# Routing split between GpSimd and VectorE, first unit turned by TensorE, and a reordered set-up in an attention and mixture-of-experts block

## The chip, the core and the metric

The kernel runs on one core of a Trainium2 chip. The core has TensorE (PE, matrix products into eight PSUM banks), VectorE (DVE), ScalarE (ACT), GpSimd (POOL, which here also issues the indirect transfers) and SyncE (SP, which issues transfers). Each engine works through its own instructions in order and waits on semaphores for the others. The metric is the device time of one execution in microseconds. One execution was recorded with a profiler, and all rows below come from it.

## What is computed

Eight sequences of 1024 tokens with 256 features go through one block. The reference, cut to what matters:

```
mod = (silu(c) @ wmod).reshape(8, 6, 1, -1);  sa, ca, ga, sb, cb, gb = mod[:, 0..5]
ga, gb = sign(g) * max(|g|, 0.25)
h = layernorm(x) * (1 + ca) + sa
x = x + ga * attention(h)          # per 64-token segment: softmax part + memory part (M, z), 16 heads
h = layernorm(x) * (1 + cb) + sb
probs = softmax(h @ router.T);  weights, indices = top_k(probs, 2);  weights /= weights.sum + 1e-6
y_e = (silu(gate) * up) @ w2[e],   gate, up = split(h @ w13[e])          # 8 experts, 256 -> 2*512 -> 256
x = x + gb * sum over the two chosen experts of weights * y_e
```

## The kernel before

**Attention.** The tokens are 64 tiles of 128 rows. A software pipeline runs over rounds: in round i every engine runs its list of stages (`program`, in `attention`), and a stage with lag n works on tile i - n. ScalarE, VectorE and GpSimd have lags of their own, so the same tile comes later in their rounds than in TensorE's. `set_up_work` puts extra work ahead of a stage in a given round, and `engine_program` walks the lists. In steady rounds all engines are filled; the first dozen rounds and the last ones are not.

**Set-up.** The six kinds of modulation come out of `wmod` in three products (`set_up_mod(e, n)`: mod0, mod1, mod2, each of 8 x 512 in f32). Each kind is split into two 16-bit halves (hi, lo) and spread over the 128 rows with small products against `of_batch` (`replicate`, 128 x 256 each). mod0, the spread of CA, mod1 and mod2 all stand ahead of the first attention tile. The spreads of B2, GA, CB and GB (32 products) stand in rounds 2 to 4 on TensorE, and the first `scores` waits for GA to be copied out of the banks that it also uses. The loads are issued at once: SyncE takes `wmod` in three pieces, x and the causal rows, ScalarE's queue the q, k and v weights, GpSimd's the router weights, masks, `wo` and the five routing tables. `scalar_weights` (line 366) turns the q, k and v weights into 16 bits once all three have landed.

**Routing.** After the last tile, VectorE ranks the experts of each token (`Part`), counts tokens per expert (`count`, line 148 writes `cnt`) and then makes 16 groups of row selectors, `rsel` (line 1247, 128 x 1024 in 16 bits, a comparison of two tensors in SBUF). TensorE uses each group for eight products (line 1344) and frees its place in a ring of four. Between group 0 and group 1 VectorE forms the tiles per expert and the slot map (lines 1252 to 1265), and after group 4 it copies `bCol`, makes `tile_at` and the eight `onto` tables (lines 1269 to 1275). Then come the table's transposes (line 1361), `tabT` (line 1285), the lookup product (line 1366) and `gidx` (line 1290), the list of rows that the gathers need. GpSimd then issues the gathers (line 1442) and SyncE the transposing transfers (line 1448) that bring a unit's rows into `xT`.

**Experts.** 75 units in 15 groups of `ORDER = "PPSPP"`: P is a pair of tiles (256 tokens), S a single tile. A pair's `gate_up` has two halves of 24 products (line 1464), its `down` has 24 (line 1541); a single has 12 in `gate_up_by_token` (line 1496) and 12 in `down`. TensorE's order in a group is p0, down(before), p1, down(p0), single, down(p1), p2, p3's first half, down(single), p3's second half, down(p2). `xT` has three places (unit u takes that of unit u - 3), gathered rows have six. GpSimd does gather(u), then scatter(u - 5), and a scatter waits until the one before it has landed. The last three chunks of `w13` (line 82, low halves) and the low halves of `w2` (line 1606, eight of them) are also made by VectorE in this stretch: the first `gate_up` waits for the former, the first `down` for the latter.

## Time and profile before

| what | us |
|---|---|
| three timed runs, median | 1270.22 |
| lowest and highest | 1270.12, 1274.2 |
| profiled execution, whole | 1279.18 |
| its span in the trace | 1277.4 |

| engine | busy in the span |
|---|---|
| TensorE products | 1129.5 us, 88% |
| weight loads | 939.8 us, 74% |
| VectorE | 895.4 us, 70% |
| ScalarE | 702.4 us, 55% |
| GpSimd | 918.1 us, 72% |

The profiled execution is 1.8 us longer than its span and 9 us longer than the median of the timed runs. The span has four stretches: set-up and filling of the pipeline (to about 60 us), attention (to about 656 us), routing (to 716 us, when the first `gate_up` starts) and the experts. A share of busy time over the whole span says little here, since each stretch has another limit. The views used are the chain that ended last, tables of stretches, and the instructions in order of time.

### The profile page before, as it was taken

What the parts mean: (1) busy time and instruction counts of PE and PEld (TensorE: products, weight loads), DVE (VectorE), ACT (ScalarE), POOL (GpSimd) and SP (SyncE); (2) the same over time, 40 slices, a digit from 0 to 9 for tenths busy, and PEclk for the clock granted to TensorE, in tenths of its full rate; (3) what the DMA queues carried; (4) which work ended last, traced back from release to release, by engine and by line L of the source; (5) the groups of instructions that cost most, each with busy time, mean ns of one, the idle gap of its engine ahead of it and who ended that gap; (6) DMA issues with size and microseconds to landing.
All of it is one profiled execution on the core that took longest, in us unless ns stands there. A gap on an engine that the chain in (4) does not pass through costs nothing. (4 is left out here: it accounts for less than half of the span.)

```text
span 1277.4 us, 52383 instructions
## 1 busy us (share of the span) xinstructions
PE 1129.5 (88%) x19163; PEld 939.8 (74%) x19163; DVE 895.4 (70%) x2388; ACT 702.4 (55%) x1407; POOL 918.1 (72%) x971
## 2 busy tenths in 40 slices
PE   4889999999999999899633499999999999999994
PEld 0677778787877777777523388888888888888883
DVE  2689999998999999999878744544444544454442
ACT  2677888888988888888633223333223323233231
POOL 3168999998999999999840457666766766677653
PEclk8699999998999999999855699999999999999997
DMA  8133344442424243333335568888897898888972
GB/s 216 47 70 82 95 137 120 117 127 88 138 84 128 88 126 100 116 109 104 113 81 183 130 117 139 139 146 147 143 134 141 141 131 132 142 157 134 133 121 33
DMA packets 214117, 154.14 MB, mean 121 GB/s; under 512 B 113339, under 2 KB 192131, under 8 KB 213747
## 3 DMA queue, kind: packets, MB, share of 16 engines
q1 hardware_dynamic: 171152, 82.25, 26.4%
q0 software_dynamic: 30720, 54.00, 26.0%
q10 hardware_dynamic: 12002, 14.54, 4.6%
q8 instruction: 167, 2.74, 1.0%
q14 instruction: 76, 0.61, 0.2%
HBM read 61.70 MB, written 43.12 MB: 82 GB/s over the span
## 5 line engine op out<-in xcount | busy, mean ns | idle before, releaser
L1464 PE MATMUL psum<-xT,xall 128*128 128x256 f16 x2880 | 327.8, 274 | 19.2 <-DMA xT<-grow 15.1
L1566 POOL DMA_INDIRECT out<-late,sidx x135 | 219.0, 1622 | 161.9 <-DVE late L1556 61.6
L1464 PEld LDWEIGHTS psum<-xT,xall 128*128 x2880 | 282.1, 98 | 55.4 <-issue 21.1
L1442 POOL DMA_INDIRECT grow<-moe_rows,gidx x135 | 145.2, 1075 | 87.1 <-DVE gidx L1290 46.3
L1472 ACT ACTIVATE sg<-psum 128x512 f32<-128x512 f32 x120 | 71.4, 595 | 223.9 <-PE psum L1464 184.9
L1477 DVE SCALAR_TENSOR_TENSOR late<-psum,sg 128x512 f32<-128x512 f32 x120 | 82.9, 691 | 150.3 <-ACT sg L1472 111.0
L1541 PE MATMUL psum<-w2s,hT 128*128 x1440 | 168.5, 274 | 3.0 <-DVE w2s L1606 2.7
L1541 PEld LDWEIGHTS psum<-w2s,hT 128*128 128x128 f16 x1440 | 141.5, 98 | 23.7 <-issue 3.5
L766 POOL TENSOR_TENSOR pT<-sc,pT 128x1024 f16<-128x1024 f32 x64 | 136.5, 2134 | 12.5 <-ACT pT L762 12.5
L1488 DVE TENSOR_TENSOR hT<-late,hT 128x512 f16<-128x512 f32 x120 | 83.2, 693 | 83.5 <-ACT hT L1484 71.0
L1484 ACT ACTIVATE hT<-late 128x512 f16<-128x512 f32 x120 | 75.6, 630 | 102.1 <-DVE late L1477 80.4
L647 PE MATMUL psum<-h1T,wqkv 128*128 128x128 f16 x1536 | 98.7, 222 | 1.0 <-DVE h1T L637 1.0
L647 PEld LDWEIGHTS psum<-h1T,wqkv 128*128 128x128 f16 x1536 | 93.4, 99 | 3.0 <-issue 1.2
L719 DVE TENSOR_REDUCE mx<-psum 128x16 f32<-128x1024 f32 x64 | 78.1, 1220 | 9.6 <-PE psum L712 8.7
L870 DVE TENSOR_TENSOR att_o<-psum,rr 64x128 f32<-64x128 f32 x256 | 73.9, 289 | 5.0 <-DVE rr L861 0.2
L922 POOL TENSOR_TENSOR xall<-xall,gat 128x256 f32<-128x256 f32 x64 | 47.1, 735 | 35.8 <-DVE gat L919 35.6
L757 ACT ACTIVATE sc<-psum 128x1024 f32<-128x1024 f32 x64 | 65.5, 1024 | 12.1 <-PE psum L750 11.4
L762 ACT ACTIVATE pT<-sc 128x1024 f16<-128x1024 f32 x64 | 67.7, 1057 | 2.0
L780 PE MATMUL psum<-mem,sig 64*64 64x68 f32 (+1 forms) x2048 | 61.6, 260 | 3.1 <-DVE sig L696 2.8
L1556 DVE SCALAR_TENSOR_TENSOR late<-psum,wrow,grow 128x256 f32<-128x256 f32 x135 | 59.4, 477 | 6.6 <-PE psum L1541 6.5
L746 PE MATMUL psum<-stk 112*64 112x64 f16 x2048 | 58.3, 199 | 5.8 <-issue 5.5
L849 PE MATMUL psum<-vs,pT 64*128 64x33 f16 x3072 | 51.1, 174 | 10.8 <-issue 8.0
(286 smaller groups left out, 2426.2 us busy)
## 6 DMA issues: line engine op xcount, KB each, us to landing
stk<-qk SPq DMA_DIRECT2D x384, 64.0 KB, 2.8
moe_rows<-hrows SPq DMA_DIRECT2D x64, 256.0 KB, 3.9
out<-xall SPq DMA_DIRECT2D x64, 128.0 KB, 3.5
raw<-in_w ACTq DMA_DIRECT2D x26, 256.0 KB, 3.4
xall<-in_x ACTq DMA_DIRECT2D x24, 256.0 KB, 4.0
raw<-in_w SPq DMA_DIRECT2D x8, 512.0 KB, 8.8
grow<-moe_rows,gidx POOLq DMA_INDIRECT x135
xT<-grow SPq DMA_TRANSPOSE x135
```

Of the source, the lines that this page charges most:

```text
L647: i = k.e.matmul(bkB[:, n * P:(n + 1) * P], wqkv[:, b_, c, n * P:(n + 1) * P], h1T[:, k.b, a, c, :], start=(c == 0 and (a, b_) == PARTS[0] ...
L719: done(k.e.tensor_reduce(mx[:, k.b, :], bkDE.rearrange("p h (n k) -> p (h n) k", k=SEG), axis=X, op=ALU.max, negate=True), "mx")
L766: done(k.e.tensor_tensor(pT[:, k.b, 1, :, :].rearrange("p n t -> p (n t)"), sc[:, k.b, :], pT[:, k.b, 0, :, :].rearrange("p n t -> p (n t) ...
L870: i = k.e.tensor_tensor(att_o[b2 * SEG:(b2 + 1) * SEG, k.b, :].rearrange("p (n w) -> p n w", w=2 * DK)[:, :, par * DK:(par + 1) * DK], de[ ...
L1442: k.e.indirect_dma_start(grow[:, k.j, q, :], None, rows_dram, at).then_inc(s_g[k.j], 16)
L1464: i = k.e.matmul(bank[:, n * LONG:(n + 1) * LONG], w13s[:, bass.ds(ex_reg * (G * 4 * I) + ((2 * c + b_) * 2 * I + col), P)], xT[:, k.x, a, ...
L1472: done(k.e.activation(sg[:, half, :], bGate[half][:, :], ACT.Silu, scale=1.0 / W_SCALE), "sg")
L1477: done(k.e.scalar_tensor_tensor(out=hf[:, half, :], in0=bUp[half][:, :], scalar=1.0 / W_SCALE, in1=sg[:, half, :], op0=ALU.mult, op1=ALU.m ...
L1484: done(k.e.activation(h_part(k, half, 0), hf[:, half, :], ACT.Copy), "hhi")
L1488: done(k.e.tensor_tensor(h_part(k, half, 1), hf[:, half, :], h_part(k, half, 0), ALU.subtract), "hlo")
L1541: i = k.e.matmul(bY[k.y][:, q * D:(q + 1) * D], hidden, w2s[:, b_, bass.ds(ex_reg * (KC * D) + n * D, D)], start=(n == 0 and (a, b_) == PA ...
L1566: k.e.indirect_dma_start(out_rows, bass.IndirectOffsetOnAxis(ap=sidx[:, n:n + 1], axis=0), yo[:, k.v, q, :], None, bounds_check=B * T - 1, ...
```

## The change

**Routing.** GpSimd forms the tiles per expert and the slot map, with its two running sums made of three shifted additions each, and makes `tile_at` and the `onto` tables; VectorE makes its 16 `rsel` groups in a row. TensorE's lookup of tile numbers moves from group 3 to group 9. ScalarE copies `bCol`, and makes half of the high parts of `w2` between the two table halves. VectorE puts four of the seven steps on `single_end` ahead of `gidx`, and the low parts of the last `w13` chunks directly behind `ex_i`.

**First unit.** Its rows are turned by eight TensorE transposes into bank 7 and one ScalarE copy, in place of two transposing transfers.

**Experts.** In each group the single's `gate_up` now comes before down(p0), p2's `gate_up` before down(p1), and p3 whole before down(single). VectorE's `weigh` calls follow. The read of a unit's expert number stands ahead of the products before it. The low halves of `w2` are made four, two and two.

**Set-up.** `wv` is loaded by SyncE behind the second piece of `wmod`. x beyond the first two segments, the causal rows and GpSimd's loads wait until q, k and v weights have landed; the five tables are issued one per round in GpSimd's rounds 10 to 14. mod2 moves to TensorE's round 2. The spreads of GA and B2 go one at a time ahead of `t1` of tiles 3 to 10, those of CB and GB ahead of `proj_v` of tiles 1 to 8, in the free halves of banks A and C; the copies out of them are eight on VectorE and eight on ScalarE, 256 wide, in place of four and four, 512 wide.

```
@@ route_vector: between the rsel groups
-            if k == 0:
-                link(e.tensor_scalar(tiles_of[:, :], cnt[:, :], (P - 1) / 2, 1.0 / P, ALU.add, ALU.mult))
...
-                for m in range(3):
-                    ins = e.tensor_copy(maps16[:, m, :, :], bc_mid(maps[0:1, m, :], P // E))
-            if k == 4:
-                e.wait_ge(s_tcol, 1)
-                link(e.tensor_copy(tile_col[:, :], bCol[:, 0:NGRP + 3]))
...
-                for i in range(NGRP):
-                    e.tensor_scalar(onto[:, i, :], number[:, 0:NW], tile_at[:, i:i + 1], None,
@@ route_gpsimd
+        def running(out, of):
+            at = of
+            for step, to in zip((1, 2, 4), (run_a[:, :], run_b[:, :], out)):
+                e.tensor_copy(to[:, 0:step], at[:, 0:step])
+                link(e.tensor_tensor(to[:, step:E], at[:, step:E], at[:, 0:E - step], ALU.add))
+                at = to
+        e.wait_ge(s_cnt, 1)
...
+        e.wait_ge(s_col, 1)
...
+            e.tensor_scalar(onto[:, i, :], number[:, 0:NW], tile_at[:, i:i + 1], None,
@@ route_scalar
+        e.wait_ge(s_tcol, 1)
+        e.activation(tile_col[:, :], bCol[:, 0:NGRP + 3], ACT.Copy).then_inc(s_col, 1)
         for half in range(2):
             e.wait_ge(s_use, NT * (half + 1))
...
+            e.wait_ge(s_2, 16 * E)
+            w2_high(range(half * 4, half * 4 + 4))
@@ the first unit
+    def x_turn_first(k):
+        k.moved(s_g, U, 0)
+        for q in range(k.nq):
+            rows = grow[:, k.j, q, 0:D].bitcast(F16)
+            for n in range(2 * G):
+                i = k.e.transpose(bTurn[:, (n * 2 + q) * P:(n * 2 + q + 1) * P], rows[:, n * P:(n + 1) * P], idh[:, :])
@@ TensorE, one group of units
+                p1.expert()
                 if before:
                     down(before)
                 gate_up(p1, 0)
+                single.expert()
                 gate_up(p1, 1)
+                gate_up_by_token(single)
+                p2.expert()
                 down(p0)
-                gate_up_by_token(single)
-                down(p1)
                 gate_up(p2, 0)
                 gate_up(p2, 1)
+                p3.expert()
+                down(p1)
                 gate_up(p3, 0)
+                gate_up(p3, 1)
                 down(single)
-                gate_up(p3, 1)
                 down(p2)
@@ set-up
         wmod_part(e, 1)
+        e.dma_start(wq32[:, :, 2 * D:3 * D], wvT.rearrange("(c p) n -> p c n", p=P)).then_inc(s_wq, 16)
         wmod_part(e, 2)
+        e.wait_ge(s_wq, 48)
         for b2 in range(2):
             x_part(e, 0, b2, slice(2, 4), s_xx)
...
+    def spread(e, n, kinds, names, bank):
+        if n == 0:
+            set_up_wait(e, "vector", "loGB")
+        part, j = divmod(n, NJ)
+        for a in range(2):
+            mm = e.matmul(bank[:, D:2 * D], of_batch[0:B, j, :], mod8s[:, a, kinds[part], :], start=(a == 0), stop=(a == 1))
...
-            set_up_wait(k.e, "vector", "GA")
+            set_up_wait(k.e, "vector", "CA23")
```

TensorE at the start of attention, before, from the first tile's q and k product on (`h` and `idf` are the first transposes, `xall,of_batch` the spreads, `mem,sig` the memory reads):

```order
8 L647 MATMUL psum<-h1T,wqkv 128x128 x24
9 L624 MATMUL psum<-idf,h 128x128
10 L625 MATMUL psum<-of_batch,shift 128x128
11 L624 MATMUL psum<-idf,h 128x128
12 L625 MATMUL psum<-of_batch,shift 128x128
13 L316 MATMUL psum<-xall,of_batch 128x256 x12
14 L780 MATMUL psum<-mem,sig 64x68 x4
15 L780 MATMUL psum<-mem,sig 64x132 x4
16 L780 MATMUL psum<-mem,sig 64x68 x4
17 L780 MATMUL psum<-mem,sig 64x132 x4
18 L656 MATMUL psum<-wqkv,h1T 128x256 x6
19 L647 MATMUL psum<-h1T,wqkv 128x128 x24
```

The same place in the changed kernel:

```order
8 L663 MATMUL psum<-h1T,wqkv 128x128 x24
9 L640 MATMUL psum<-idf,h 128x128
10 L641 MATMUL psum<-of_batch,shift 128x128
11 L640 MATMUL psum<-idf,h 128x128
12 L641 MATMUL psum<-of_batch,shift 128x128
13 L320 MATMUL psum<-xall,cs 8x512 x2
14 L797 MATMUL psum<-mem,sig 64x68 x4
15 L797 MATMUL psum<-mem,sig 64x132 x4
16 L797 MATMUL psum<-mem,sig 64x68 x4
17 L797 MATMUL psum<-mem,sig 64x132 x4
18 L673 MATMUL psum<-wqkv,h1T 128x256 x6
19 L663 MATMUL psum<-h1T,wqkv 128x128 x24
```

The twelve spreads ahead of the first memory reads have gone, and the two products of mod2 (`xall,cs`) stand there.

VectorE in the routing, before, from the end of the slot map to the copy of the turned table:

```order
1567 L1265 CAST maps<-maps 1x128 x3
1568 L1247 TENSOR_TENSOR rsel<-count,wqkv 128x1024 x4
1569 L1269 COPY tile_col<-psum 128x11
1570 L1271 TENSOR_SCALAR tile_at<-tile_col 128x8
1571 L1272 SCALAR_TENSOR_TENSOR tile_at<-tile_col,tile_at 128x8
1572 L1275 TENSOR_SCALAR onto<-number,tile_at 128x135 x8
1573 L1247 TENSOR_TENSOR rsel<-count,wqkv 128x1024 x11
1574 L1278 TENSOR_SCALAR ex_of<-iota,tend 128x75
1575 L1280 SCALAR_TENSOR_TENSOR ex_of<-iota,tend,ex_of 128x75 x6
1576 L1282 TENSOR_SCALAR past<-iota,tend 128x75
1577 L1283 TENSOR_TENSOR ex_of<-ex_of,past 128x75
1578 L1285 COPY tabT<-psum 128x1024
```

VectorE in the changed kernel, from the end of the placing on:

```order
1560 L169 CAST wqkv<-row 128x32
1561 L1269 TENSOR_TENSOR rsel<-count,wqkv 128x1024 x16
1562 L1277 TENSOR_SCALAR ex_of<-iota,tend 128x75
1563 L1279 SCALAR_TENSOR_TENSOR ex_of<-iota,tend,ex_of 128x75 x6
1564 L1281 TENSOR_SCALAR past<-iota,tend 128x75
1565 L1282 TENSOR_TENSOR ex_of<-ex_of,past 128x75
1566 L1284 COPY tabT<-psum 128x1024
1567 L1274 SCALAR_TENSOR_TENSOR ex_of<-iota,single_end,ex_of 128x75 x4
1568 L1287 CAST found<-psum 128x135
```

The map and the `onto` tables no longer stand between the `rsel` groups. GpSimd in the changed kernel holds their end, ahead of the first gathers (`grow`):

```order
725 L1393 TENSOR_TENSOR moved<-single_end,odd 128x8
726 L1394 TENSOR_TENSOR maps<-moved,tend 128x8
727 L1396 CAST maps<-maps 1x128 x3
728 L1400 TENSOR_SCALAR tile_at<-tile_col 128x8
729 L1401 TENSOR_TENSOR tile_at<-tile_at,tile_col 128x8
730 L1402 TENSOR_SCALAR tile_at<-tile_at,tile_col 128x8
731 L1404 TENSOR_SCALAR onto<-number,tile_at 128x135 x8
732 L1479 DMA grow<-moe_rows,gidx 128x520 x11
```

Before, GpSimd had nothing between the end of attention and these gathers.

## Rows read from the trace of the kernel before

**Rows 1.** The chain that ended last, shares of the span by line.
```profile
by line: PE psum L1464 23.7%; PE psum L1541 13.3%; PE psum L1496 3.0%; issue 1.2%; DMA out<-late,sidx 1.1%; POOL out L1566 0.6%; DVE rsel L1247 0.6%; DMA xT<-grow 0.5%; DVE w2s L1606 0.3%; DMA grow<-moe_rows,gidx 0.3%; DVE ex_of L1280 0.1%;
```

**Rows 2.** Stretches of the set-up: from:to, length, busy times, PEclk, DMA share, GB/s.
```profile
0.00:8.00 8.00, 1.94 (x3) 0.39 (x4) 0.17 (x1) 1.50 (x2) 7.38 (x29) 1.00 0.65 171
8.00:14.00 6.00, 3.51 (x10) 0.98 (x8) 2.32 (x9) 2.24 (x5) 0.00 (x0) 1.00 1.06 305
14.00:28.00 14.00, 6.39 (x8) 0.86 (x8) 2.92 (x11) 1.75 (x3) 1.27 (x2) 0.89 1.04 263
30.00:44.00 14.00, 11.98 (x96) 8.78 (x97) 8.16 (x21) 8.18 (x15) 1.90 (x3) 0.50 0.10 30
```

**Rows 3.** Set-up, in order of time: start, us, engine, line, what [idle before <-releaser].
```profile
6.06 3.57 PE L310 MATMUL psum<-xall,cs 128*8 128x512 f32 x4 [6.06 <-DMA xall<-in_wmod]
...
26.64 1.48 ACT L366 ACTIVATE wqkv<-xall 128x1536 f16<-128x1536 f32 x1 [10.64 <-DMA xall<-in_wvT]
...
36.65 2.74 PE L316 MATMUL psum<-xall,of_batch 8*128 8x256 f16 x12
...
48.87 0.59 ACT L663 ACTIVATE qk<-psum 128x512 f16<-128x512 f32 x1
...
52.77 1.61 PE L780 MATMUL psum<-mem,sig 64*64 64x68 f32 x32 [2.44 <-DVE sig L696]
```

**Rows 4.** Routing and first units, in order of time.
```profile
676.31 0.17 DVE L148 TENSOR_TENSOR cnt<-seen,start 128x8 f32<-128x8 f32 x1
...
681.34 0.69 DVE L1247 TENSOR_TENSOR rsel<-count,wqkv 128x1024 f16<-128x1024 f16 x1
...
688.26 1.41 DVE L1275 TENSOR_SCALAR onto<-number,tile_at 128x135 f16<-128x135 f16 x8
689.58 6.71 DVE L1247 TENSOR_TENSOR rsel<-count,wqkv 128x1024 f16<-128x1024 f16 x11
...
696.20 0.26 DVE L1278 TENSOR_SCALAR ex_of<-iota,tend 128x75 f32<-128x75 f32 x1
...
696.88 0.59 PE L1361 MATMUL psum<-idh,tab 128*128 128x128 f16 x4
...
697.57 7.67 ACT L1331 ACTIVATE w2s<-raw 128x1024 f16<-128x1024 f32 x8
...
699.06 0.69 DVE L1285 COPY tabT<-psum 128x1024 f16<-128x1024 f16 x1
...
701.80 0.23 DVE L1290 TENSOR_SCALAR gidx<-rowf 128x135 int32<-128x135 f32 x1
...
702.90 1.09 POOL L1442 DMA_INDIRECT grow<-moe_rows,gidx  x1 [46.26 <-DVE gidx L1290]
...
707.86 23.93 SPq L1448 DMA_TRANSPOSE xT<-grow  x9
708.05 3.49 DVE L82 SCALAR_TENSOR_TENSOR xall<-late,xall 128x1024 f16<-128x1024 f32 x3
...
716.01 13.19 PE L1464 MATMUL psum<-xT,xall 128*128 128x256 f16 x96 [15.12 <-DMA xT<-grow]
...
727.04 4.63 DVE L1606 SCALAR_TENSOR_TENSOR w2s<-raw,w2s 128x1024 f16<-128x1024 f32 x4
...
731.92 4.23 PE L1541 MATMUL psum<-w2s,hT 128*128 x24 [2.71 <-DVE w2s L1606]
```

**Rows 5.** GpSimd's cheapest and usual operations: one line's durations (ns min/median/max), one group.
```profile
L606 POOL TENSOR_TENSOR nmr<-nmr,rstd x16: 192/204/218, 17.2 to 559.9; 128x4 f32<-128x4 f32 x16
...
L922 POOL TENSOR_TENSOR xall<-xall,gat 128x256 f32<-128x256 f32 x64 | 47.1, 735 | 35.8 <-DVE gat L919 35.6
```

**Rows 6.** Experts: one stretch; waits (us in total, times, longest); a piece of the chain.
```profile
750.00:1250.00 500.00, 495.89 (x4370) 426.51 (x4368) 241.35 (x517) 152.99 (x253) 330.07 (x247) 1.00 0.85 138
...
POOL out L1566 <- DMA out<-late,sidx: 49.3, 22, 5.9
...
960.56 1.05 issue
```

288 lines of the change are left out of this document (162 added, 126 removed).

## The prediction

> **What bounds the kernel now.** I first read the chain that ended last [rows 1]. Its named pieces are nearly all products of the expert stretch. Attention does not show in it because there the engines pass work back and forth; I take that stretch as unchanged, since neither the stages nor their order in the steady rounds are touched. The table of stretches then shows that TensorE is busy for 495.89 of 500 us between 750 and 1250 us at full clock [rows 6], so a new order of the same products can give back at most 4.1 us there. That leaves two places where TensorE stands still and the change acts: the set-up, where attention cannot begin before the q, k and v weights are there at 26.64 us (ScalarE idle 10.64 us, released by the load of `wv`), and the stretch from the count at 676.31 us to the first `gate_up` at 716.01 us, before which TensorE waited 15.12 us [rows 3, 4].
>
> **Set-up, the weights.** From 14 to 28 us the 16 DMA engines are full (share 1.04, 263 GB/s) [rows 2]: the weights wait behind other loads, not behind their own. Counting bytes from the shapes: before `wv` can land, the changed kernel needs two pieces of `wmod` (0.52 MB each), eight pieces of x (0.13 MB each), the three weights (0.26 MB each) and 0.12 MB of small ones, 3.0 MB, or 3.5 MB if the third `wmod` piece runs beside. Before, 8 us at 171 GB/s and 6 us at 305 GB/s moved 1.37 + 1.83 = 3.2 MB by 14 us [rows 2]. So 3.0 to 3.5 MB is there at 13.4 to 15.1 us. I take 14.5, which is 12.1 us sooner than 26.64. Bounds: a gain of 9 (fewer queues at work, slower rate) to 13.
>
> **Set-up, the rest.** mod2 now stands in the first busy rounds. Its four passes take 3.6 us as mod0's did at full clock [rows 3], but between 30 and 44 us the granted clock was 0.50, the lower of the two levels (1.2 GHz) [rows 2], where they take up to 7.1 us. Twelve spreads (2.74 us) leave the same place, so the first memory read comes 0.9 to 4.4 us later. Against that, the wait of the first `scores` for GA goes, and ScalarE no longer stops for the CB spreads before it reads the second tile's q and k, which it did until 48.87 us; TensorE's next memory read at 52.77 us had waited 2.44 us for what follows from that [rows 3]. I work the chain through: mod2, hi parts, `h1T`, q and k of tile 1, sigma of tile 1. It puts that read 15.5 to 16.7 us after the end of the first tile's q and k product, where it stood about 17.2 us after it. Gain 1 (bounds -3 and +5). The spreads are as many as before (32 products), but their copies are 16 of 256 columns instead of 8 of 512; on VectorE and ScalarE that puts about 0.4 us into each of eight rounds that are no longer idle, and GpSimd's five table issues sit ahead of its stages. The same work was done before in stalls that vanish. I take a loss of 1.6, with 0 and 6 as bounds. The SyncE queue gets the causal rows and eight x pieces behind the wait for the weights; the first segment stacks queue behind them, due some 9 us later, so I cost this at nothing; if they took more than that, `scores` of tile 0 would be late by the excess. **Set-up in all: 12.1 + 1 - 1.6 = 11.5 us sooner** (bounds 5 and 15).
>
> **Routing, VectorE.** The 11 later `rsel` groups take 6.71 us, 0.61 each. Sixteen in a row from 681.34 us end at 691.1, and the next work starts there and not at 696.20: 5.1 us sooner [rows 4]. That work, nine small operations, runs from 696.20 to 699.06, 2.86 us, so to 694.0. Beside it ScalarE makes four of the `w2` copies (7.67 / 8 = 0.96 each, 3.8 us) ahead of the second table half; if the `w2` loads are there by mid-stream this ends about 2 us after TensorE's last use. Table half (0.6), transposes (0.59), `tabT` (0.69) then end at 695.4. From the end of `tabT` at 699.75 to the start of `gidx` it was 2.05 us; four `ex_of` steps (0.32 each, 1.3) now stand beside the 1.1 us of the lookup product and add 0.2. `gidx` is done at 697.9, where it was 702.03: 4.1 us sooner.
>
> **Routing, GpSimd.** Before, GpSimd was idle for 46.26 us here [rows 4], so no row shows it at this work beside VectorE. It gets 25 operations of at most 8 columns (128 in three of them), then 3 more and the 8 `onto`. The nearest row below is 0.20 us (4 columns) and above 0.735 us (256 columns) [rows 5]. From the count (676.5) to the tenth `rsel` group (687.4), behind which TensorE now stops for the map, there are 10.9 us, 0.44 for each of 25. At 0.20 plus the wait for its own semaphore they take 6 to 7 us and nothing waits. The `onto` tables, 0.2 to 0.735 each, take 1.6 to 5.9 us from about 688.5, due at 695.4; I take 0.45, 3.6, hidden. If this cover is gone, each late microsecond counts in full. VectorE's `rsel` compares two tensors in SBUF, and GpSimd's operations read SBUF too. That the two wait for one another is possible, with no row for or against. I take 1.1 us off for it. The Trainium skill, "SBUF — State Buffer", Who interferes with whom, says that a VectorE instruction with two SBUF inputs contends with a GpSimd instruction that reads SBUF, and that the one that starts later is fully blocked; no run here shows it yet. By that rule the case is the first rival, below. **Routing: 3.0 us sooner** (bounds +4.5 and -5).
>
> **First unit.** From `gidx` done (702.03) to the rows in place (707.86, when the transposing transfers start) it was 5.8 us, and to the first `gate_up` 14.0 us [rows 4]. The 5.8 stay. Instead of the transfers come eight transposes (four take 0.59, so 1.2), one ScalarE copy of 1024 columns (0.96 to 1.05, by the `w2` copies) and three hand-overs of 0.1: 8.3 us. 5.7 us sooner. `gate_up` also needs the low parts of `w13`: 3 ex_of steps, `ex_i` and 3.49 us, done 4.8 us after `gidx`. What is late next is the low part of `w2`, needed by the first `down`. Before, TensorE had done four half units in 13.19 us and then waited 2.71 us [rows 4]. VectorE's list after `gidx` is: 4.8, index work 3.8, row weights 0.4, four `w2` (4.63), first pair, two `w2` (2.3), second pair (each half about 2.1 once ready), two `w2` (2.3): 28 us after `gidx`. TensorE has then finished the single's 12 products too, at 8.3 + 13.1 + 2.6 = 24.0, and waits about 4 us. Before, `down` began 29.9 us after `gidx`; now 28.1, with 2.6 us more work behind it. 1.8 + 2.6 = **4.4 us sooner** (bounds 2 and 6).
>
> **The groups.** The stalls in the steady groups, such as 1.05 us at 960.56, stand between p2 and p3, where two `gate_up` follow each other and p3's first half needs the banks that p2's first half filled; down(p1) now stands between. Of 4.1 us at most [rows 6] I take 1.5, since GpSimd's scatters are chained nearly as tightly as TensorE and end the kernel. Bounds 0 and 4.
>
> **Sum.** 11.5 + 3.0 + 4.4 + 1.5 = 20.4 us. The span 1277.4 becomes 1257.0 and the profiled execution 1279.2 becomes 1258.8. The timed median was 9 us under the profiled execution; taking the same 20.4 us off gives 1270.2 - 20.4 = **1249.8 us**.
>
> **Rival 1: the map is late.** If each GpSimd operation first waits out an `rsel`, it takes 0.20 + 0.61 = 0.81 us, and 25 take 20.3 us: ready at 696.8, 9.4 us behind TensorE. The ring then stops VectorE too. Against it: 4.8 of the first 10.9 us lie beside short operations, not `rsel`. It decides from 0.44 us an operation. At 0.81 it takes about 9 us of the gain: 1259. Chance 0.10. The skill's rule named above would give this time.
>
> **Rival 2: little comes of the set-up.** Weights at 18 instead of 14.5, or mod2 at the low clock and 0.4 us more in each filling round with nothing given back: 5.5 us instead of 11.5, so 1256. For it is the clock of 0.50 [rows 2]; against it the idle 10.64 us. Chance 0.13.
>
> **Rival 3, slower: p2's rows come late in every group.** p2 takes the place in `xT` that p0 frees. With the new order p2 is multiplied 2.6 us sooner after p0. Its gather is issued behind the scatter of the group before's single, whose `down` ends 2.6 us later in its group. The room shrinks by 5.2 us. Scatters wait for the one before 22 times, on average 2.2 us and at most 5.9 [rows 6]. I estimate the room at about 10 us now, so some 5 are left at the mean; at 5.9 us all the time about 1 is left, and slower transfers (DMA share 0.85) could use it up. It turns the sign from 20.4 / 14 = 1.5 us in each of 14 groups; at 2 us it costs 28 us: 1278. Against it is the short stretch of idle TensorE in the same place now. Chance 0.07.
>
> **How the numbers follow.** Forecast as summed: 0.68, own range 1242 to 1257 from the bounds taken together. Better by all upper bounds, about 1240: 0.02. The rivals: 0.10, 0.13, 0.07. What a measurement can tell from no change is 0.3%, 3.8 us. The first four cases are faster by more: 0.91 after leaving 0.02 of them to within 0.3%. Slower: 0.07. The range that should hold 8 in 10 leaves out rival 3 and some of the edges: 1239 to 1261.
>
> **What would show it.** Right: the weights' conversion on ScalarE at 13 to 16 us; the second tile's memory read near 40 us; `rsel` as one run of some 10 us; the map ready before the tenth group; gap from `gidx` to the first `gate_up` near 8.3 us; TensorE idle about 4 us before the first `down`, released by `w2` on VectorE; no stall between p2 and p3. Wrong: the conversion after 18 us; `rsel` operations longer than 0.61 us or GpSimd's longer than 0.44; TensorE waiting at the lookup of tile numbers; waits at p2's first product, released by `xT`.

## The result, and the profile after

The changed kernel takes 1253.67 us (median of 4 runs, 1250.14 to 1256.63), the kernel before 1272.21 in the same job (1270.12 to 1280.91): ratio 0.9841, 95% interval 0.9805 to 0.9876. Between the medians it is faster by 18.5 us; forecast were 20.4. The ratio is not that of the two medians: by it the gain is 20.2 us. In a later job both stood on one chip again (kernel `a_again` below): 1251.77 against 1267.16, 15.4 us between the medians, ratio 0.9885 (0.9851 to 0.9918), by it 14.6 us. The two intervals meet between 0.985 and 0.988, at 16 to 19 us.

The profiled execution of the changed kernel took 1250.14 us (span 1248.2), 29 us under that of before. That pair is misleading: before's was 9 us over its median, and part of it lies in attention, whose steady rounds the change doesn't touch. So no term below rests on these two profiles alone.

Set-up after, three stretches of the table (columns as in [rows 2]), the third 500 us of the experts from 30 us behind the first `gate_up`:

```profile
14.00:28.00 14.00, 8.79 (x39) 3.97 (x37) 7.74 (x20) 8.20 (x13) 7.65 (x10) 1.00 0.82 182
30.00:44.00 14.00, 12.01 (x285) 9.63 (x289) 10.73 (x27) 9.46 (x21) 3.14 (x6) 1.00 0.41 87
718.71:1218.71 500.00, 499.73 (x4414) 431.57 (x4413) 246.88 (x524) 155.38 (x255) 336.04 (x251) 1.00 0.84 140
```

And in order of time, as in [rows 3] (L373 is the weights' conversion, L640 the first tile's transposes, L320 mod2, L797 the memory reads of the first and the second tile):

```profile
15.76 1.48 ACT L373 ACTIVATE wqkv<-xall 128x1536 f16<-128x1536 f32 x1 [1.96 <-DMA xall<-in_wkT]
...
19.76 0.45 PE L640 MATMUL psum<-idf,h 128*128 128x128 f32 x1 [3.57 <-POOL h L631]
...
22.07 2.72 PE L663 MATMUL psum<-h1T,wqkv 128*128 128x128 f16 x24 [1.02 <-DVE h1T L653]
...
25.51 1.88 PE L320 MATMUL psum<-xall,cs 128*8 128x512 f32 x4
...
30.13 0.92 PE L797 MATMUL psum<-mem,sig 64*64 64x68 f32 x32 [2.75 <-DVE xall L437]
...
36.07 0.92 PE L797 MATMUL psum<-mem,sig 64*64 64x68 f32 x32 [1.60 <-DVE sig L713]
```

The weights are there 10.9 us sooner than in [rows 3], and the second memory read starts 16.7 us sooner. 324 products run in the two stretches, 104 in [rows 2]. The chain that ended last is still made of the expert products, as in [rows 1]:

```profile
by line: PE psum L1511 25.1%; PE psum L1588 14.4%; PE psum L1543 2.9%; issue 0.6%; PE psum L1346 0.5%; POOL onto L1404 0.4%; POOL out L1613 0.4%; DMA grow<-moe_rows,gidx 0.3%; DMA out<-late,sidx 0.3%; DVE w2s L1661 0.3%; DVE late L1524 0.2%
```

New in it are GpSimd's `onto` tables, 0.4% or 5 us.

Routing and the first units after, in order of time; the rows that answer to [rows 4]:

```profile
655.83 0.17 DVE L149 TENSOR_TENSOR cnt<-seen,start 128x8 f32<-128x8 f32 x1
...
656.10 0.20 POOL L1383 TENSOR_SCALAR tiles_of<-cnt 128x8 f32<-128x8 f32 x1 [19.93 <-DVE cnt L149]
...
660.96 10.02 DVE L1269 TENSOR_TENSOR rsel<-count,wqkv 128x1024 f16<-128x1024 f16 x16
661.18 0.52 POOL L1393 TENSOR_TENSOR moved<-single_end,odd 128x8 f32<-128x8 f32 x1
...
662.38 2.02 POOL L1396 CAST maps<-maps 1x128 f16<-1x128 f32 x3
...
668.36 1.52 POOL L1400 TENSOR_SCALAR tile_at<-tile_col 128x8 f32<-128x8 f32 x1 [3.96 <-ACT tile_col L1327]
...
671.29 5.16 POOL L1404 TENSOR_SCALAR onto<-number,tile_at 128x135 f16<-128x135 f16 x8
...
673.97 0.69 DVE L1284 COPY tabT<-psum 128x1024 f16<-128x1024 f16 x1 [0.20 <-PE psum L1363]
...
676.61 1.06 PE L1368 MATMUL psum<-onto,tabT 128*128 128x135 f16 x8 [2.74 <-POOL onto L1404]
...
678.64 0.23 DVE L1290 TENSOR_SCALAR gidx<-rowf 128x135 int32<-128x135 f32 x1
...
685.55 1.03 PE L1492 MATMUL psum<-idh,grow 128*128 128x128 f16 x8 [7.88 <-DMA grow<-moe_rows,gidx]
686.68 1.02 ACT L1496 ACTIVATE xT<-psum 128x1024 f16<-128x1024 f16 x1 [9.69 <-PE psum L1492]
...
688.71 13.57 PE L1511 MATMUL psum<-xT,xall 128*128 128x256 f16 x96 [2.13 <-ACT xT L1496]
...
702.12 2.75 PE L1543 MATMUL psum<-xall,xT 128*128 x12
...
707.25 2.35 DVE L1661 SCALAR_TENSOR_TENSOR w2s<-raw,w2s 128x1024 f16<-128x1024 f32 x2
...
709.85 5.01 PE L1588 MATMUL psum<-w2s,hT 128*128 x24 [4.98 <-DVE w2s L1661]
```

The map is ready at 664.4, 3.2 us before TensorE gets to its lookup at 667.58. The `onto` tables are not ready in time: they start at 671.29 and take 0.65 us each on GpSimd, where VectorE took 0.18 [rows 4], so the lookup product starts 1.95 us behind the end of `tabT`. From the start of the count's last step to the end of `gidx` it is 23.04 us, before 25.72. The first `down` still waits for the low halves of `w2`, and now 4.98 us.

### The profile page after: what moved, and what is told of

It reads as the page before. It is cut to its first block and busy times, and to the rows that moved or that the text cites. A ratio compares the mean times of both kernels' runs of the same rounds, so it can differ in the third digit from the quotient of the medians.

```text
span 1248.2 us, 52449 instructions
## 1 busy us (share of the span) xinstructions
PE 1122.4 (90%) x19171; PEld 934.3 (75%) x19171; DVE 895.6 (72%) x2370; ACT 704.3 (56%) x1414; POOL 932.0 (75%) x1007
## 5 line engine op out<-in xcount | busy, mean ns | idle before, releaser
L797 PE MATMUL psum<-mem,sig 64*64 64x68 f32 (+1 forms) x2048 | 58.7, 252 | 4.4 <-DVE xall L437 2.7
L927 PE MATMUL psum<-wo,aT 128*128 128x256 f16 x384 | 56.2, 286 | 2.5 <-ACT aT L919 2.5
```

## The experiments

All ratios are against the kernel before on the same chip, with 95% intervals, and a gain in us beside a ratio is worked out from it. Since timed medians move from job to job (the kernel before from 1267.16 to 1272.21, the changed one from 1251.77 to 1253.67), each is read with three distances from its profile: the place of GpSimd's residual addition of tiles 0, 6 and 63 (set-up and attention), the stretch from the count's last step to the end of `gidx`, and that from there to the first `down`.

| kernel | tile 0 | tile 6 | tile 63 | count to gidx | gidx to down | down to end |
|---|---|---|---|---|---|---|
| before | 85.27 | 140.79 | 648.90 | 25.72 | 29.89 | 545.5 |
| after | 69.82 | 125.11 | 628.43 | 23.04 | 30.98 | 538.4 |
| a_again | 72.72 | 127.47 | 631.10 | 23.71 | 29.28 | 538.7 |
| e_setup | 70.39 | 126.91 | 632.38 | 25.72 | 29.79 | 547.8 |
| e_rest | 85.63 | 139.26 | 642.99 | 23.72 | 30.98 | 539.8 |
| e_loads | 79.81 | 133.68 | 637.78 | 25.73 | 29.62 | 542.7 |
| e_mod2 | 69.34 | 125.23 | 629.27 | 23.70 | 30.95 | 538.5 |
| e_oldloads | 82.83 | 138.74 | 644.60 | 23.03 | 30.04 | 537.6 |
| e_group | 69.55 | 124.59 | 628.26 | 23.71 | 29.70 | 554.2 |
| e_onto | 70.73 | 126.07 | 627.95 | 22.85 | 28.88 | 538.4 |
| e_map | 72.56 | 127.66 | 628.05 | 25.80 | 29.60 | 538.2 |
| e_noturn | 73.35 | 128.55 | 631.38 | 23.05 | 33.41 | 541.3 |
| e_w2 | 69.61 | 124.94 | 626.83 | 23.09 | 24.90 | 535.7 |
| e_best | 72.62 | 127.80 | 630.00 | 21.50 | 24.66 | 538.6 |

### The two halves apart

`e_setup` is the kernel before with all of the diff's set-up part, `e_rest` with all of its routing and expert part.

> The kernel before with the whole new set-up and its old routing and experts. Theory A (the set-up gives more than forecast, because TensorE's products run short about 20 us sooner): the first segment's memory read of round 7 stands 16 us sooner than before (106.3 to 90.0 us, as in the changed kernel) and the time is 15 to 17 us under the kernel before, ratio 0.987 to 0.988. Theory B (the forecast, 11.5 us): ratio 0.991; the 5 us more in the profile of the changed kernel would then be the luck of one profiled execution of before, 9 us over its median. The weights' conversion on ScalarE stands at 15 to 16 us by both.

> The kernel before with its old set-up and all of the new routing, first unit and order of the groups. Theory A: set-up and rest add up, and the traces show 2.7 us sooner at gidx and 6 us sooner from there to the end, so 8 to 9 us under the kernel before, ratio 0.993. Theory B: the timed medians differ by 18.5 us only; if the set-up gives 16, the rest gives 2 to 3 us, ratio 0.998. Forecast: 8.9 us, ratio 0.993.

`e_setup`: 1261.51 against 1270.64, ratio 0.9927 (0.9899 to 0.9954), 9.3 us. `e_rest`: 1266.73, ratio 0.9959 (0.9933 to 0.9986), 5.2 us (1.8 to 8.5). Together 14.5 us, beside 14.6 and 20.2 of the changed kernel: the halves add up as far as this can be told. Theory A for the set-up falls by the time. The 16 us of the profile shrink on the way: 15 at tile 0, 12.3 at tile 6, 10.6 at tile 63, against `e_rest`, which has the old set-up. That is one pair of profiles, though; by the means over all profiles with the new and with the old set-up the distance is 14.2, 13.5 and 16.6 us, so a loss behind tile 6 is not shown. `e_rest` shows also how far a profile of the same code strays: it has before's set-up and attention and is 5.9 us ahead of before's profile at tile 63.

### What shortened the set-up

Four kernels, each with one part. `e_loads`: the order of loads alone, on the kernel before.

```
+        e.dma_start(wq32[:, :, 2 * D:3 * D], wvT...)      # SyncE, behind wmod piece 2
         wmod_part(e, 2)
+        e.wait_ge(s_wq, 48)                               # SyncE, ahead of x beyond segment 2
...
+        e.wait_ge(s_wq, 48)                               # GpSimd, ahead of its loads
         for dst, src in later_loads:
```

> The kernel before with the order of its loads alone changed: wv behind the second piece of wmod, x beyond the first two segments, causal rows and GpSimd's loads behind the weights. mod2, the spreads and the tables' place in the program are as before. Theory A: the conversion of the weights comes 10 to 11 us sooner (at about 16 us instead of 26.6), TensorE's spell of slow products (2.7 us for the 24 of a q and k product instead of 1.5) ends sooner by as much, and the time falls by 10 to 11 us, ratio 0.992; the 12 spreads ahead of the first memory read still cost 2.7 us. Theory B: mod2 ahead of the first tile holds TensorE until the third piece of wmod has landed, the first product of q and k waits for it, and the gain is 5 us or less.

1264.89, ratio 0.9955 (0.9930 to 0.9980), 5.7 us. That is near the amount of theory B, but by neither theory's mechanism: the weights come at 15.95, yet the first transposes wait for something else.

```profile
15.95 1.49 ACT L369 ACTIVATE wqkv<-xall 128x1536 f16<-128x1536 f32 x1 [1.93 <-DMA xall<-in_wkT]
...
23.23 1.09 ACT L613 ACTIVATE h<-xall,nmr,rstd 128x256 f32<-128x256 f32 x2 [5.79 <-POOL nmr L609]
...
41.87 0.60 ACT L386 ACTIVATE mods<-psum 128x512 f32<-128x512 f32 x1 [4.48 <-PE psum L319]
...
43.19 0.58 ACT L666 ACTIVATE qk<-psum 128x512 f16<-128x512 f32 x1
```

I had put GpSimd's wait and its nine loads ahead of its first stages, and ScalarE waited 5.79 us for GpSimd's `nmr` behind them. So the first transposes start at 24.85 (before 30.64, after 19.76). In the changed kernel the loads stand in GpSimd's tenth round, and the tables one to a round: half of what the earlier weights are worth hangs on that. The second thing is below it: ScalarE stops 4.48 us for a CB spread and only then reads the second tile's q and k, at 43.19; the second memory read comes at 47.09, 22.2 us behind the first transposes, as before (22.1), though many products around it run short. In the changed kernel it is 16.3.

`e_oldloads` keeps the new places of mod2 and the spreads, with the old loads; `e_mod2` is the changed kernel with mod2 back ahead of the first tile.

```
     def tensor_third(e):                                   # e_mod2: in tensor_first again
-        set_up_mod(e, 2)
```

> The changed kernel with the old order of loads (wv third on ScalarE's queue, x, causal rows and all of GpSimd's loads at once); mod2 and the spreads stay in their new places. It asks what shortened the way from the first tile's transposes to the second memory read from 22.1 us to 16.3. Theory A (the spreads, and ScalarE's and VectorE's stops for them): it stays at 16 to 17.5 us though the weights come at 26.6 and TensorE idles for them, and the first rounds are 10 to 11 us later than in the changed kernel at the end of set-up; ratio 0.993. Theory B (TensorE's clock, 0.50 in that stretch before): it goes back to 20 us or more.

> The changed kernel with mod2 back ahead of the first tile; the new loads and spreads stay. Theory A: the wait for the third piece of wmod, which now lands behind wv, costs little, since TensorE idles for the weights anyway, and mod2 no longer stands (1.88 us) between the first q and k products and the first memory read: within 2 us of the changed kernel, ratio 0.983 to 0.985 against before. Theory B: the move of mod2 is what brought the 5 us above the forecast: ratio 0.988.

`e_oldloads`: 1262.75 against 1267.16, ratio 0.9956 (0.9936 to 0.9976), that is what `e_rest` has, so the new spreads alone give nothing that can be timed. Its rows, and behind them those of `a_again`, which is the changed kernel itself:

```profile
30.57 0.45 PE L638 MATMUL psum<-idf,h 128*128 128x128 f32 x1 [10.72 <-POOL h L629]
...
36.57 2.73 PE L318 MATMUL psum<-xall,cs 128*8 128x512 f32 x4
```

```profile
19.86 0.45 PE L640 MATMUL psum<-idf,h 128*128 128x128 f32 x1 [3.91 <-POOL h L631]
...
25.87 2.64 PE L320 MATMUL psum<-xall,cs 128*8 128x512 f32 x4
...
38.54 0.92 PE L797 MATMUL psum<-mem,sig 64*64 64x68 f32 x32 [1.56 <-DVE sig L713]
```

From the first transposes to the second memory read: 18.8 us in `e_oldloads` (read at 49.37), 18.7 in `a_again`, 16.3 in the profiles of after, `e_mod2` and `e_w2`, 16.5 in `e_setup`. So 3.3 us of the 5.8 come from the spreads and the stops for them, shown by the old loads with the new spreads; the other 2.4 us come and go between executions of the same code, with TensorE's pace: mod2 takes 1.88 us in one and 2.64 in the other, and between 30 and 35 us the granted clock is 1.00 in after and 0.66 in `a_again`. The ten profiles with the new set-up fall into these two levels, six at 16.3 to 16.6 us and four at 18.6 to 18.9. `e_mod2`: 1255.27, ratio 0.9897 (0.9857 to 0.9936), which fits both theories (0.983 to 0.985 and 0.988); the profile decides. Its first memory read comes 9.1 us behind the first transposes, against 10.4 to 11.6 with mod2 in its new place, but the second at the same 16.3, and tile 0 is 0.5 us sooner than after. By the profiles the place of mod2 is worth nothing. At tile 6 `e_oldloads` is only 0.5 us ahead of `e_rest`, from 2.8 at tile 0: the rounds that carry the spreads give it back.

### Routing

`e_onto`: `tile_at` and `onto` on VectorE behind the sixteenth `rsel`. `e_map`: the map as well, between the `rsel` groups as before.

```
@@ route_vector (e_onto), taken out of route_gpsimd
+        e.wait_ge(s_col, 1)
+        link(e.tensor_scalar(tile_at[:, :], tile_col[:, 0:NGRP], whole, step, ALU.is_ge, ALU.mult))
...
+            e.tensor_scalar(onto[:, i, :], number[:, 0:NW], tile_at[:, i:i + 1], None, ALU.is_equal)
```

> The changed kernel with tile_at and the eight onto tables back on VectorE, in one piece behind the sixteenth rsel group; GpSimd keeps the map. In the changed kernel the lookup product waited 2.74 us for GpSimd's onto tables, which took 5.16 us beside VectorE where VectorE took 1.41. Theory A (GpSimd's small operations are stretched by VectorE's): the tables are ready before tabT, the lookup product starts 0.1 us behind tabT, and gidx is 1.6 to 1.9 us sooner after the count (21.0 us instead of 22.8). Theory B: VectorE, now with 1.7 us more ahead of ex_of, makes tabT late by as much, and nothing is gained. On the time 1 to 2 us of 1254, under what the timing can tell.

> The changed kernel with the whole slot map and the onto tables back on VectorE between the rsel groups and the lookup of tile numbers behind group 3, as before; all the rest as in the changed kernel. Theory A: GpSimd takes 5.1 us off VectorE's line and gives 2.4 us of it back as wait for its tables, so gidx comes 2.5 to 3 us later after the count than in the changed kernel (25.4 us instead of 22.8), time up by 2 to 3 us. Theory B (contention is large): rsel runs faster with GpSimd idle, 0.60 us instead of 0.63 each, and the loss is under 1.5 us.

```profile
670.98 1.41 DVE L1283 TENSOR_SCALAR onto<-number,tile_at 128x135 f16<-128x135 f16 x8
...
675.16 0.69 DVE L1292 COPY tabT<-psum 128x1024 f16<-128x1024 f16 x1
...
675.91 1.09 PE L1376 MATMUL psum<-onto,tabT 128*128 128x135 f16 x8 [2.73 <-DVE tabT L1292]
```

`e_onto`: 1250.26 against 1269.16, ratio 0.9852 (0.9822 to 0.9881). The tables take 1.41 us instead of 5.16 and the product starts 0.06 us behind the end of `tabT`, but `tabT` itself now stands behind `ex_of` and is 1.7 us late (it ended 18.8 us behind the count in after, 20.5 here). So 22.85 us instead of 23.03 to 23.72 (two levels, explained below): both theories hold in part, and the gain is 0.2 to 0.9 us. `e_map`: 1251.90, ratio 0.9869 (0.9838 to 0.9901). Its 25.80 us against 23.04 and 23.71 are the worth of GpSimd's share, 2.1 to 2.8 us, a little under theory A's 2.5 to 3; 25.80 is also what the kernel before has (25.72), so the other edits of the routing bring nothing up to `gidx` by themselves. With GpSimd idle `rsel` takes 6.71 / 11 = 0.61 us, with it 10.02 / 16 = 0.626. The difference lies in three of the sixteen, which start 0.69 us apart instead of 0.60, beside GpSimd's three copies of the map (662.38 to 664.40). Against theory B, VectorE hardly pays for the sharing. The times can't tell these kernels apart; the profiles do.

### First unit

`e_noturn`: the first unit's rows by two transposing transfers again.

```
-            x_turn_first(unit(e, 0))          # TensorE
-            x_copy_first(unit(e, 0))          # ScalarE
-                if k and u > 0:
+                if k:                          # SyncE
                     x_trans(k)
```

> The changed kernel with the first unit's rows brought by two transposing transfers on SyncE, as before, in place of the eight products and the copy. Theory A: the first gate_up comes later (14 us after gidx instead of 9.8), but VectorE's list of low halves of w2 ends when it did, about 30 us after gidx, because it waits for the products only in part: of 4.2 us, 2 to 4 us reach the first down and the end. Theory B: the first down is set by the w2 low halves alone, and the time doesn't change (within 0.5 us at the first down).

1256.66, ratio 0.9892 (0.9863 to 0.9920). The first `gate_up` starts 14.12 us after `gidx` instead of 9.84, the first `down` 33.41 after it instead of 29.28 to 30.98: 2.4 to 4.1 of 4.3 us arrive, as in theory A. The time can't tell it from the changed kernel (0.9841 and 0.9885).

`e_w2` asks for the wait before the first `down`. It changes VectorE's order alone:

```
+            w2_low(range(E))                   # all eight, behind the last w13 chunks
...
                 hidden(p0, 1)
+                if group == 0:
+                    index_work(e)              # oh_tile ... sidx, 11 operations
+                    row_weights(p0)
```

> The changed kernel with one order changed on VectorE: all eight low halves of w2 directly behind the last w13 chunks, and the list of scatter rows (15 operations, 3.8 us) and the first row weights behind the first pair's hidden halves. Theory A (TensorE's 5.0 us before the first down is VectorE's list): the low halves are done 14 us after gidx instead of 30.7, the first down starts behind the single's twelve products, 26 us after gidx instead of 31.0, with no wait for w2, and the time falls by 4 to 5 us (ratio 0.981). Theory B (the products are the limit): the first pair's hidden halves come later behind 4.6 us more of w2, the second half of p1 waits for its bank, and less than 2 us is won.

1249.09 against 1267.16 (`a_again` beside it 1251.77), ratio 0.9843 (0.9812 to 0.9873).

```profile
681.76 9.17 DVE L1664 SCALAR_TENSOR_TENSOR w2s<-raw,w2s 128x1024 f16<-128x1024 f32 x8
...
687.11 12.70 PE L1514 MATMUL psum<-xT,xall 128*128 128x256 f16 x96 [2.12 <-ACT xT L1499]
...
699.64 2.75 PE L1546 MATMUL psum<-xall,xT 128*128 x12
...
702.23 2.78 PE L1591 MATMUL psum<-w2s,hT 128*128 x24
```

The wait is gone and the first `down` starts 24.9 us after `gidx`. And its 24 products take 2.78 us at a granted clock of 1.00, where they took 5.01 behind the wait of 4.98, at 0.50: the stop had cost twice. By the profile the gain is 4.4 to 6.1 us up to the first `down` and some 3 us behind it; the medians say 2.7 and the ratios 5.3, with intervals that overlap, so that the size isn't settled by timing. The profiled execution, 1239.83 us, is also the fastest of its six, 9 us under their median.

### The groups

`e_group`: the old order of products on TensorE and of `weigh` on VectorE, the reads of the expert numbers as in the change.

```
                 gate_up(p1, 1)
+                down(p0)
                 gate_up_by_token(single)
-                down(p0)
+                down(p1)
                 gate_up(p2, 0)
                 gate_up(p2, 1)
-                down(p1)
                 gate_up(p3, 0)
-                gate_up(p3, 1)
                 down(single)
+                gate_up(p3, 1)
```

> The changed kernel with the old order of products in a group on TensorE and of weigh on VectorE; the reads of the expert numbers stay ahead. Theory A (the stalls between p2 and p3 are what the new order removes): between 30 and 530 us behind the first gate_up TensorE is busy 496 of 500 us instead of 499.7, and the time is 3.5 to 4 us over the changed kernel. Theory B (the early reads of the expert numbers do it): TensorE stays busy for over 499 us and the time is the same within 1 us.

1252.83, ratio 0.9864 (0.9835 to 0.9894): by the time no difference from the changed kernel. Its profiled execution is the slowest of its seven, 1265.23, and shows where such an execution loses its time. TensorE in 500 us of the experts, from 30 us behind the first `gate_up`, for `e_group`, then `e_setup` (old order) and `a_again` (new order):

```profile
719.11:1219.11 500.00, 487.46 (x4294) 418.52 (x4293) 237.34 (x509) 151.25 (x247) 325.24 (x248) 1.00 0.86 138
```

```profile
729.05:1229.05 500.00, 493.14 (x4338) 423.14 (x4337) 240.60 (x516) 153.72 (x252) 331.53 (x247) 1.00 0.85 138
```

```profile
721.98:1221.98 500.00, 499.66 (x4413) 431.35 (x4411) 245.79 (x525) 155.88 (x254) 331.32 (x252) 1.00 0.83 139
```

The waits of `e_group` in this stretch (us in total, times, longest), TensorE's first, then GpSimd's, and behind them GpSimd's in the changed kernel:

```profile
PE psum L1511 <- DMA xT<-grow: 11.0, 7, 3.3
```

```profile
POOL out L1613 <- DMA out<-late,sidx: 87.4, 42, 5.7
```

```profile
POOL out L1613 <- DMA out<-late,sidx: 51.2, 21, 4.9
```

Of its 12.5 us of idle TensorE 11.0 are waits for rows in `xT`: here GpSimd waited for scatters twice as often as in the changed kernel, its gathers came late, and so did the rows. That is no stall of the order, so this profile doesn't price it. The other three with the old order have 495.48 (before), 495.85 (`e_loads`) and 493.14 us busy; ten with the new one 497.7 to 500.0, the changed kernel among them with 499.73 and 499.66. The groups themselves tell the same: from ScalarE's first copy for the single of the second group to that of the fifteenth it is 464.7 to 466.4 us in the three and 459.4 to 463.0 in the ten. I read 4 to 5 us from that; the timed pair (1252.83 against 1251.8 to 1253.7 for the changed kernel) doesn't confirm it.

### What a better order gives

`e_best` is `e_w2` with `tile_at` and `onto` on VectorE, `tabT` ahead of the last half of the first `ex_of` steps, and all steps on `single_end` behind `gidx`.

```
+        by_pair(range(1, 4))
         e.wait_ge(s_made, 3)
         e.tensor_copy(tabT[:, :, :], ...).then_inc(s_tabT, 1)
+        by_pair(range(4, E - 1))
...
         e.tensor_scalar(gidx[:, :], rowf[:, :], 0.0, None, ALU.max).then_inc(s_idx, 1)
-        by_single(range(4, E - 1))
+        by_single(range(0, E - 1))
```

> The kernel of the run before it with, in addition, tile_at and the onto tables on VectorE behind the sixteenth rsel group, tabT ahead of half of the first ex_of steps, and all steps on single_end behind gidx. Theory A: with the tables back, only the place of tabT holds up the lookup product (VectorE made tabT 1.2 us late behind ex_of in the kernel with onto alone moved); gidx comes 21.5 to 22 us after the count instead of 23.0 to 23.7, and with the 5 us from w2 the time is 6 to 7 us under the changed kernel, about 1246, ratio 0.980. Theory B: the twelve other ex_of steps behind gidx delay the first gate_up by the w13 low halves and give the routing's gain back.

> The changed kernel unchanged, so that the other kernels of this job stand beside it on one chip: ratio 0.985 against before, routing from the count to gidx 23.0 to 23.7 us, first down 31.0 us after gidx.

```profile
673.02 1.41 DVE L1283 TENSOR_SCALAR onto<-number,tile_at 128x135 f16<-128x135 f16 x8
...
675.63 0.69 DVE L1292 COPY tabT<-psum 128x1024 f16<-128x1024 f16 x1
...
676.38 1.09 PE L1381 MATMUL psum<-onto,tabT 128*128 128x135 f16 x8 [1.11 <-DVE tabT L1292]
...
703.55 2.78 PE L1593 MATMUL psum<-w2s,hT 128*128 x24
```

1242.46 against 1267.16, ratio 0.9797 (0.9765 to 0.9828); the changed kernel in the same job 0.9885 (0.9851 to 0.9918). These intervals don't meet: it beats both kernels, the changed one by 9 us between the medians and 11 by the ratios. From the count to `gidx` it is 21.50 us and from there to the first `down` 24.66, together 6.8 us less than in `a_again`, within the 6 to 7 us expected. All seven steps on `single_end`, four more than in the change, now stand behind `gidx` (not twelve more, as expected above), and they hold up nothing: the first `gate_up` comes 9.0 us after `gidx`, in `a_again` 9.8.

## Why the prediction was right, and where it wasn't

The time and the sign were right: 1249.8 forecast, 1253.67 measured, 20.4 us against 18.5 and 15.4 between the medians. That the sum came so close is in part luck: set-up and groups gave more than forecast in the profiles, routing and first unit less. The own range of 1242 to 1257 doesn't follow from the bounds either; added one by one they reach from 1241 to 1268. By its steps, each measured by the stage (means over all profiles that have the part: for set-up the residual addition of tile 6, 140.0 in two with all of the old set-up against 126.6 in nine with all of the new; for the groups TensorE's busy time in 500 us, 494.8 against 499.2; for the first unit the first `down`, 29.77 us after `gidx` in three profiles of the old kind against 30.10 in the seven with both the turned rows and the new order, and the 2.6 us of work behind it):

| term | forecast | measured |
|---|---|---|
| weights there | 12.1 (14.5 us) | 10.9 (15.76 us) |
| set-up in all | 11.5 | 13.5 in profiles, 9.3 timed |
| count to gidx | 3.0 | 2.35 |
| gidx to first gate_up | 5.7 | 4.2 |
| first unit in all | 4.4 | 2.3 |
| groups | 1.5 | about 4 in profiles |

**Weights.** The bytes counted gave 13.4 to 15.1 us; the last of the three weights to land was k's, at 15.76, not v's, so it wasn't the queue of the moved load. 1.2 us late.

**Set-up, the rest.** The mechanism was right (fewer stops of ScalarE before the second tile's q and k), its size wasn't: +1 was taken, with +5 as a bound; the runs show 3.3 us from the spreads. I had the second memory read 15.5 to 16.7 us after the end of the first q and k product; it is 11.3 us in after and 13.7 in `a_again`. The step that failed is mod2's price: I put it at 3.6 to 7.1 us, since I took mod0's 3.6 us for TensorE's full pace. In its new place it took 1.88 to 2.85 us; 3.57 is the price at the lower level, as the last section shows. The first memory read still came 1.3 to 2.5 us later behind the first transposes (9.1 before), inside the 0.9 to 4.4 forecast, but for another reason: TensorE is done with mod2 at 27.39 and then waits 2.75 us for VectorE, which works on mod2's results. That this number fits is luck. The loss of 1.6 us by later rounds is there: 14.2 to 16.7 us at the second memory read are 13.5 at tile 6. What I named in one sentence without a price, that GpSimd's tables stand ahead of its stages, was the larger matter: badly placed, GpSimd's loads cost 5.1 us in `e_loads`.

**Routing.** Sixteen `rsel` in 10.02 us, as forecast. GpSimd's map took 0.18 to 0.26 us an operation beside VectorE's short ones (once 0.35) and 0.52 to 0.67 beside `rsel`: 8.3 us in all, 0.33 each, where the first rival decides from 0.44. 20 of the 25 were through before the first `rsel` got in their way. What followed was mis-sized: the three `tile_at` steps took 1.52, 0.47 and 0.68 us, and the tables 0.65 each for 0.45. They were due at the end of `tabT` and late by 1.95 us. The length of the tables alone would not have done it, since I had covered up to 5.9 us for the eight and they took 5.16. But I had them start 7.2 us after the first `rsel`, and they started 10.3 us after it, behind the `tile_at` steps.

The first of these steps is the costly one, and it has two lengths: 1.52 us in four profiles (after, `e_oldloads`, `e_noturn`, `e_w2`) and 2.91 to 2.92 in the four others (`a_again`, `e_rest`, `e_mod2`, `e_group`). These are the four with 23.03 to 23.09 us from the count to `gidx` and the four with 23.70 to 23.72. From `a_again`, that step, and the last two tables:

```profile
671.02 2.92 POOL L1400 TENSOR_SCALAR tile_at<-tile_col 128x8 f32<-128x8 f32 x1 [3.96 <-ACT tile_col L1327]
```

```profile
L1404 POOL TENSOR_SCALAR onto<-number,tile_at x2: 617/620/622, 678.6 to 679.2; 128x135 f16<-128x135 f16 x2
```

The step stands beside a run of `rsel` on VectorE. The two after it, behind the end of that run, take 0.20 and 0.35 us. If 0.20, 0.20 and 0.35 are taken as GpSimd's own price, the three steps are stretched by 1.9 us in after and 2.7 in `a_again`, and the lookup product is late by 1.95 and 2.71. That is an account from rows; no run has these steps on GpSimd with `rsel` elsewhere. The two tables above stand beside an idle VectorE (from 678.44 to 681.11), so 0.62 us is GpSimd's own price at 135 columns, and little of the 0.65 comes from VectorE at work beside it.

**Rival 1** was right about contention and wrong about what it hits: beside `rsel` most operations took 0.52 to 0.67 us, not 0.81, on the map nothing waited, and the tables were late instead. So the two signs named for it, `rsel` over 0.61 us and GpSimd's operations over 0.44, did show, and the loss was 2 to 3 us at the lookup product instead of the 9 priced. The Trainium skill, "SBUF — State Buffer", Who interferes with whom, says that of a VectorE instruction with two SBUF inputs and a GpSimd one that reads SBUF the later is blocked in full. By these rows the direction agrees: 8 columns on GpSimd go from 0.20 to 0.52 us, and for the first `tile_at` step to 1.52 or 2.92, more than one `rsel`. But VectorE, which by the rule would be blocked whenever it comes second, lost 0.016 us on each `rsel` in the mean and 0.1 at most; and its six `ex_of` steps, which have two inputs in SBUF too, take 1.96 us beside GpSimd's tables, as they did before without them. That side of the rule these rows don't bear out.

**First unit.** Three hand-overs were taken at 0.1 us. The last one, from ScalarE's copy to the first `gate_up`, takes 1.0 us (687.70 to 688.71). In the trace TensorE's sequencer loads the unit's expert number there, from 687.74 to 688.23, and computes with it until 688.65: for the first unit this read stands behind the wait. The gather was seen 0.8 us later on TensorE than on SyncE. Then the first `down`: forecast 28.1 us after `gidx`, measured 28.9 to 31.0, 30.1 in the mean, which with 2.6 us more work behind it makes the 2.3 of the table. The list on VectorE was right in its order; I had it end at 28 and it ended at 30.7, as `gate_up` came 1.5 us later. What I left out is that TensorE runs slowly behind such a wait (5.01 us for 24 products at a granted clock of 0.50, 2.78 without the wait at 1.00).

**Groups.** I took 1.5 of 4.1 us because GpSimd's scatters seemed nearly as tight as TensorE. In the profiled executions with the new order they mostly aren't; TensorE is idle for 0.3 of 500 us after.

**Rival 2** did not come: the weights were there before 18 us. **Rival 3** did not either: the changed kernel waits at most 0.3 us for `xT` in 500 us of the groups, and the most in a kernel with the new order is 2.3 us (`e_noturn` and `e_best`). Rows that come late are real, though: `e_group`'s profile shows them in one execution, 11.0 us in 7 waits, and `e_best`'s 2.5 us in 2. But `e_group` has the old order, so this is not the room that rival 3 has the new order take away.

Still open: the terms by stage add up to 13.5 + 2.35 + 2.3 + 4 = 22.2 us, and the timed runs give 15 to 20. `e_rest` and `e_setup` come out lower timed than by their stages as well (5.2 for 8.7, 9.3 for 13.5, which is above the 12.8 that the interval of `e_setup` allows). Each stage was seen in two to ten profiled executions. What takes the difference back, or whether two profiles with the old set-up are too few, these runs don't tell.

## What to carry to other kernels

When loads are full, count the bytes ahead of the one that everything waits for; but then look at which engine issues the loads put back and what stands behind them, since a wait there can eat half the gain. Small serial work is well placed on an idle GpSimd as long as it has slack beside VectorE's long operations (a step of 0.2 us took 1.5 to 2.9 there); what is due at a fixed point (here eight tables of 135 columns) is cheaper on VectorE, placed behind the copy that the next engine waits for. Before a first product, make everything that it needs and nothing that is needed later: in the profiles the order of one list on VectorE was worth at least as much as the whole routing change, in the times 2.7 to 5.3 us.

## What the runs showed of the hardware

**The clock column reads 1.00 where nothing is recorded.** In the changed kernel's profile it stands at 1.00 from the first product on, and yet mod0 takes 3.57 us and the first 24 q and k products 2.72, as long as the same 24 before at a granted clock of 0.50 (1.2 GHz, [rows 2]); ten microseconds later 24 take 1.50. But this trace has no clock record ahead of 24.9 us, and the column shows 1.00 for want of one. In `e_group` the records begin at 8.4 us, and there the same 24 products stand at 0.50:

```profile
21.80:24.60 2.80, 2.78 (x25) 2.65 (x25) 0.91 (x3) 2.40 (x5) 1.80 (x4) 0.50 0.98 187
```

```profile
21.82 2.72 PE L663 MATMUL psum<-h1T,wqkv 128*128 128x128 f16 x24 [1.02 <-DVE h1T L653]
```

So the slow pace at the start is that of the lower level, and four passes of a modulation product cost 3.57 us there and 1.88 at the upper one. `a_again` bears it out: its first record, at 1.00, begins at 27.4 us, and mod2 runs from 25.87 to 28.51. The 1.53 us before and the 1.11 us after make 1.53 / 3.57 + 1.11 / 1.88 = 1.02 of a mod2. I had read mod0's 3.6 us as the fast price because the column said 1.00, and doubled it for the slow one. Where a duration is to be carried over, take it from a row of known pace.

**A stop of TensorE can be paid twice.** Behind the wait of 4.98 us the first `down` ran almost wholly at the lower level, 5.01 us for 24 products; in `e_w2`, without the wait, the level stayed and they took 2.78. The stretches, from after and from `e_w2`:

```profile
709.00:712.00 3.00, 2.15 (x11) 1.57 (x12) 1.75 (x5) 1.23 (x2) 0.00 (x0) 0.50 0.00 0
```

```profile
702.00:705.00 3.00, 3.00 (x28) 2.57 (x27) 1.80 (x3) 2.07 (x4) 0.00 (x0) 1.00 0.23 44
```

With waits of 3.8 to 6.7 us nine profiles have 4.1 to 5.3 us there. With 2.71 us it went both ways: 4.23 before and 4.40 in `e_setup`, both partly at the lower level, and 2.81 in `e_loads`, at the upper.

**In attention the lower level turns up at other places in each execution, and most of what it costs comes back.** Before, between 290 and 300 us (columns as in [rows 2]):

```profile
290.00:295.00 5.00, 5.00 (x97) 3.67 (x90) 3.41 (x9) 4.05 (x6) 3.33 (x5) 0.62 0.35 96
295.00:300.00 5.00, 5.00 (x91) 4.17 (x85) 3.95 (x14) 2.40 (x8) 3.91 (x6) 0.70 0.32 96
```

The granted clock is at its lower level for part of two such pieces, TensorE is then busy all the time, and the residual additions of tiles 23 and 24 are 11.25 us apart instead of mostly 8.5 to 9.4. In `e_setup` this happened at 125 and 179 us, in the changed kernel at 219 and 325, in `e_w2` at 219, in `e_mod2` nowhere between 35 and 600. What set it off isn't shown. Two profiles of one attention code differ by up to 6 us at its end (before and `e_rest`), and these pieces are not the main part of it: before is 3.0 us behind `e_rest` at tile 20, 5.9 at tile 24 and 3.5 again at tile 30. `e_map` and `e_oldloads`, which have no such piece between 60 and 600 us, still differ by 5.5 us between tiles 6 and 60 (481.9 and 487.4). Where that scatter comes from is open.
